# Deform stage of a four-layer convolution kernel: who copies the gather indices, and what GpSimd waits for between tiles

## The reference, cut to what matters

```python
offset = _conv2d(x, offset_w)                     # [B, 2*9, H, W]
sy = base_y + off[:, :, 0];  sx = base_x + off[:, :, 1]
y0, x0 = floor(sy), floor(sx);  ly, lx = sy - y0, sx - x0
p =     corner(y0,     x0,     (1 - ly) * (1 - lx))   # a gather per pixel and tap,
p = p + corner(y0,     x0 + 1, (1 - ly) * lx)         # zero outside the image
p = p + corner(y0 + 1, x0,     ly * (1 - lx))
p = p + corner(y0 + 1, x0 + 1, ly * lx)
y = jnp.einsum('bckhw,ock->bohw', p, wk)
attn = sigmoid(mean(y) + std(y));  return y * attn    # per image and channel
```

## Time and profile before

| what | before |
| --- | --- |
| median of three runs | 15070.81 us |
| the profiled execution's own time | 15021.82 us |
| its span | 15020.2 us |
| GpSimd busy, whole span | 7518.3 us (50%) |
| TensorE matmul, VectorE, ScalarE busy | 8857.2, 6520.5, 3085.6 us |
| indirect gathers (L1786) | 7056, 6823.6 us busy, 4426.0 us idle in front of them |
| granted TensorE clock, mean | 0.733 |

### The profile page before, as it was taken

The page is one execution under the profiler, slowest core; times in us unless marked ns, Lnnn a source line. Parts: engine busy times, 40 slices in busy tenths (PEclk is TensorE's granted clock), DMA queues, the critical chain, the costliest instruction groups (busy, mean ns, idle before and its releaser), DMA issues.

```text
span 15020.2 us, 156851 instructions
## 1 busy us (share of the span) xinstructions
PE 8857.2 (59%) x51639; PEld 6070.3 (40%) x51639; DVE 6520.5 (43%) x13120; ACT 3085.6 (21%) x5214; POOL 7518.3 (50%) x7657
## 2 busy tenths in 40 slices
PE   6897888888554544545454545454454545454543
PEld 2333444448443433333343434343343434343433
DVE  5655556553334444343434343434434343434333
ACT  3433444432111111111111111111111111111111
POOL 0011222212466666666666666666666666666665
PEclk9998999989666666767676766666666657676766
DMA  3322111126333333333333333333333333333332
GB/s 95 84 82 66 52 60 56 56 99 189 96 91 109 91 108 99 101 99 101 106 96 103 98 109 91 109 91 109 99 102 102 98 103 96 104 98 109 91 94 83
DMA packets 503924, 1436.05 MB, mean 96 GB/s; under 512 B 128980, under 2 KB 234196, under 8 KB 474576
## 3 DMA queue, kind: packets, MB, share of 16 engines
q0 software_dynamic: 353344, 970.88, 22.2%
q1 hardware_dynamic: 150032, 458.00, 10.1%
HBM read 1175.46 MB, written 252.90 MB: 95 GB/s over the span
## 4 chain that ended last, share of the span: by engine, by line
POOL 29%; issue 19%; DMA 13%; DVE 8%; PE 6%; another core or an unknown queue 0%; DVEq 0%; POOLq 0%; ACT 0%; ACTq 0%; SPq 0%
POOL e_g L1786 29%; DMA e_g<-table_dram,e_index_slots 12%; DVE e_g L2050 2%; PE e_ps L1903 2%; DVE e_g L2052 2%; PE e_ps L1918 2%; PE e_ps L1930 2%; PE e_ps L1939 1%; DMA e_tmp<-x3s_dram 1%; DVE e_x3t L1963 1%; DVE e_index_slots L2024 1%; DVE e_x3t L1967 0%; DVE e_w_next L2008 0%; DVE e_st L1971 0%
## 5 line engine op out<-in xcount | busy, mean ns | idle before, releaser
L1786 POOL DMA_INDIRECT e_g<-table_dram,e_index_slots x7056 | 6823.6, 967 | 4426.0 <-issue 1893.4
L1930 PE MATMUL e_ps<-k_ident,e_g 128*128 128x128 f32 x7056 | 1719.1, 398 | 4897.7 <-DVE e_g L2052 4840.2
L1930 PEld LDWEIGHTS e_ps<-k_ident,e_g 128*128 128x128 f32 x7056 | 1153.8, 197 | 5455.4 <-DVE e_g L2052 5209.6
L1939 PE MATMUL e_ps<-e_corners,e_w_def 128*64 128x128 f32 x14112 | 2667.5, 369 | 268.6 <-issue 148.9
L2024 DVE COPY e_index_slots<-e_index_now 128x9 uint32<-128x9 uint32 (+1 forms) x784 | 137.9, 177 | 5866.8 <-DMA e_g<-table_dram,e_index_slots 4314.5
L1939 PEld LDWEIGHTS e_ps<-e_corners,e_w_def 128*64 128x64 f32 x14112 | 2430.1, 197 | 463.7 <-issue 319.0
L1855 ACT ACTIVATE e_corners<-e_ps 128x512 f32<-128x512 f32 (+1 forms) x2352 | 1064.7, 489 | 4603.2 <-PE e_ps L1930 3895.9
L2049 DVE TENSOR_TENSOR e_ps<-e_g,e_ps 128x512 f32<-128x512 f32 (+1 forms) x2352 | 1324.5, 563 | 115.6 <-DMA e_g<-table_dram,e_index_slots 61.1
L2052 DVE TENSOR_TENSOR e_g<-e_g,e_ps 128x512 f32<-128x512 f32 (+1 forms) x2352 | 1301.5, 553 | 81.3
L2050 DVE TENSOR_TENSOR e_g<-e_g,e_ps 128x512 f32<-128x512 f32 (+1 forms) x2352 | 1284.8, 546 | 0.0
L1860 ACT ACTIVATE e_big<-e_ps 64x128 f32<-64x128 f32 (+1 forms) x784 | 211.8, 270 | 3518.7 <-remote 2210.0
(11 more groups left out here) (438 smaller groups left out, 8075.1 us busy)
## 6 DMA issues: line engine op xcount, KB each, us to landing
e_g<-table_dram,e_index_slots POOLq DMA_INDIRECT x7056
table_dram<-e_rt SPq DMA_DIRECT2D x32, 1624.0 KB
a_xt<-x_in SPq DMA_DIRECT2D x16, 1568.0 KB
v_dram<-a_vout SPq DMA_DIRECT2D x32, 784.0 KB, 8.5
b_xt<-v_dram SPq DMA_DIRECT2D x16, 1568.0 KB
v_dram<-b_vout SPq DMA_DIRECT2D x32, 784.0 KB, 7.5
c_v2t<-v_dram SPq DMA_DIRECT2D x16, 1568.0 KB
c_xt<-x_in SPq DMA_DIRECT2D x16, 1568.0 KB, 6.6
```

Source lines behind the costliest of these rows:

```text
L1786: pool.indirect_dma_start(out=g[:, slot, tap * CORNERS:(tap + 1) * CORNERS], out_offset=None, in_=table, in_offset=bass.IndirectOffsetOnAx ...
L1930: mm = pe.transpose(ps[:, TURN[tap // 4], (tap % 4) * P:(tap % 4 + 1) * P], g[:, slot, tap * CORNERS:tap * CORNERS + 2 * C], k.ident[:, :])
L1939: mm = pe.matmul(ps[0:C, OUT, 0:P], w_d[:, tap, :], corners[:, tap, :], start=(tap == 0), stop=(tap == TAPS - 1))
```

## The change

VectorE no longer copies indices. GpSimd has a new function, take: it copies the 9 indices of the tile itself, from index_now to index_slots, waits for its own copy (index_ready), and issues the nine gathers. The wait for the landing of the previous tile's gathers is gone. What used to follow from VectorE's copies is now said directly: GpSimd waits for bank_done of the tile that used the slot 7 tiles ago (as before), at a pair's first tile for the positions of that pair (switched at 3p), and after a pair's first group for the switch that follows the end of the pair before (switched at 3p + 2). GpSimd's one loop over 111 groups becomes a first group, a loop over the first pair's other groups, and a loop over the 15 other pairs with a loop over groups in it.

```diff
+                def take(r, slot, start):
+
+                    pool.tensor_copy(index_slots[:, slot, :], at(index_now, start, TAPS)).then_inc(index_ready, 1)
+                    pause(pool, index_ready, r * SLOTS + (slot + 1), passed)
+                    gather(slot)
+
+                pool.wait_ge(switched, 2)
                 for slot in range(SLOTS):
-                    pool.wait_ge(index_ready, slot + 1)
-                    if slot:
-                        pool.wait_ge(gathered[slot - 1], 16 * TAPS)
-                    gather(slot)
-                with pool.Fori(1, PAIRS * GROUPS) as r:
+                    take(0, slot, slot * TAPS)
+                with pool.Fori(1, GROUPS) as group:
                     for slot in range(SLOTS):
 
-                        pool.wait_ge(bank_done, (r - 1) * (3 * SLOTS) + (3 * slot + 3))
-                        pool.wait_ge(gathered[(slot - 1) % SLOTS], r * (16 * TAPS) + (16 * TAPS if slot else 0))
-                        pause(pool, index_ready, r * SLOTS + (slot + 1), passed)
-                        gather(slot)
+                        pause(pool, bank_done, (group - 1) * (3 * SLOTS) + (3 * slot + 3), passed)
+                        take(group, slot, group * GK + slot * TAPS)
+                with pool.Fori(1, PAIRS) as p:
+                    for slot in range(SLOTS):
+
+                        if slot == 0:
+                            pool.wait_ge(switched, p * 3)
+                        pause(pool, bank_done, (p * GROUPS - 1) * (3 * SLOTS) + (3 * slot + 3), passed)
+                        take(p * GROUPS, slot, K3 + slot * TAPS)
+                    pause(pool, switched, p * 3 + 2, passed)
+                    with pool.Fori(1, GROUPS) as group:
+                        for slot in range(SLOTS):
+
+                            pause(pool, bank_done, (p * GROUPS + group - 1) * (3 * SLOTS) + (3 * slot + 3), passed)
+                            take(p * GROUPS + group, slot, group * GK + slot * TAPS)
@@ positions, VectorE
                         switch(0)
-                        for slot in range(SLOTS):
-                            issue(slot, slot * TAPS)
@@ turn, VectorE
-                def issue(slot, start):
-
-                    dve.tensor_copy(index_slots[:, slot, :], at(index_now, start, TAPS)).then_inc(index_ready, 1)
@@
                         dve.wait_ge(gathered[slot], r * (16 * TAPS) + 16 * TAPS)
-                        if not last:
-                            issue(slot, group * GK + (GK + slot * TAPS))
```

## The result

The changed kernel takes 15874.01 us (median of four runs, 15852.92 to 15891.92) against 15067.99 us beside it: a ratio of 1.0536, with a 95% interval of 1.0518 to 1.0554. It is slower by 806 us where 1431 us were to be gained. The profiled execution took 15878.16 us, its span 15876.5.

A forecast was written before the change was run, and what follows sets the result against it. GpSimd was taken as the bound, by its nine gather issues and the pause between tiles. 15021.8 profiled - 2390 removed + 963 added = 13595, plus 49 for the runs' median: 13640 us, range 13010 to 14030.

The forecast's parts named there:

- What bounds before, and what the change removes: GpSimd's gathers and the pause between tiles bound the kernel; removing the landing wait at 783 steps saves 2390 us.
- What it adds: At each of 783 tile steps GpSimd now spends 1.23 us (0.42 to 1.70), in all 963 us.
- 0.15, 0.18 and 0.90 us: Parts of the new step: ninth gather's end to copy, the copy itself, copy's end to the next tile's first gather.
- The shared access to SBUF: VectorE instructions with two SBUF inputs could hold GpSimd's copies: nought in the sum, 16 us on the high end.
- What is late next. GpSimd still: After the change GpSimd takes 597 us a pair and stays last; VectorE's 280 and TensorE's 349 leave slack.
- The first, a landing wait in another form: GpSimd cannot issue past gathers in flight, so the step stays 3.05 us and the time 15070; chance 0.06.
- The second, the lead used up at a pair's end: GpSimd cannot get ahead at 15 pair ends, so 590 us return and the time is 14230; chance 0.05.
- The third: GpSimd pays 1.66 us per change between copy and gather; step 4.55 us, time 16245, slower; chance 0.05.
- What would show it: Gathers of 0.946 us spaced 1.25, steps near 1.2 alike everywhere, a copy near 0.2, VectorE still waiting for landings.
- two signs named for an error upward: In GpSimd's trace: the step exceeds 1.7 us, or gathers stretch while more than nine are in flight.

The follow-up runs named there:

- the kernel with four fills: Changed kernel plus four fills of 256 floats on GpSimd before each tile's copy; repeated over five runs: 14375.23 us, ratio 0.9517 to the kernel before.
- the first run with four fills: Changed kernel plus four fills of 256 floats on GpSimd before each tile's copy, measured the first time: 14348.39 us against 15082.36.
- the kernel before without any copy on GpSimd: Kernel before with GpSimd's wait for the previous tile's landing taken away, VectorE still copying the indices: 15954.09 us against 15042.58.
- the second probe: Kernel before plus, at its end, 180 TensorE records beside direct transfers from two queues, quarter-byte gathers and fills; 92 records in 10 us beside SyncE's transfers.
- the probe: Kernel before plus, at its end, 180 TensorE records beside gathers spaced by fills: pace breaks after 16 us at 1.33 us, 21 at 1.38, not at 1.44.

## Why the prediction was wrong, point by point

**What bounds before, and what the change removes: right.** GpSimd's step of 2.73 us was the bound, and it went. **What it adds: right within its ends.** Of 0.15, 0.18 and 0.90 us, in sum 1.23, the trace shows 0 (the copy starts where the ninth gather ends, 9042.78 + 0.96 = 9043.74), 0.20 and 0.81, in sum 1.01. **The shared access to SBUF** did not matter: a gather is 972 ns in the mean and was 967.

**The step that failed** is "What is late next. GpSimd still". It gave TensorE slack by its 349 us of busy time in a pair, a figure taken while the gathers came every 1.53 us in a usual tile. The change itself moved that to 1.34, and at 1.34 TensorE does not keep its pace: the changed kernel's gathers start from 3865.1 to 15820.0 us, 747 us a pair and not 597. So the sum was made for an engine that stays off the path, and the stage is now set by TensorE, through ScalarE (one weights bank for each group) and VectorE. GpSimd's gain is spent in its waits for bank_done. Why it comes out above the kernel before and not just level is argued from rows and not tried by itself: TensorE falls behind until GpSimd has filled its seven slots and stops, as it did for 28.98 us before 9031.66, and gets its pace back only in such stops; at 9058.15 it releases the next bank 2.33 us into GpSimd's idleness.

Could a row of the kernel before have warned? Of its timeline at the tile of the earlier trace rows, and, as the last row, the same matmuls of the kernel with four fills:

```profile
9022.56 3.02 PE L1939 MATMUL e_ps<-e_corners,e_w_def 128*64 128x128 f32 x18
9027.78 0.27 ACT L1860 ACTIVATE e_big<-e_ps 64x128 f32<-64x128 f32 x1 [4.56 <-remote]
...
9032.86 3.00 PE L1957 MATMUL e_ps<-e_corners,e_w_def 128*64 128x128 f32 x18
```

The matmuls of the kernel before are modelled to end at 9025.58; ScalarE is let go 2.20 us later, and the releaser is "remote". So a modelled end cannot be taken at its word. But that is no sign of a slowed TensorE yet: in the kernel with four fills, which keeps its pace, the modelled end is 9035.86 and ScalarE is let go at 9037.45, 1.59 us later. On the pages, "remote" ends 2210.0 of the 3518.7 us of idle time in front of this store before, 1996.6 of 3513.6 us in the first run with four fills, and 4534.7 of 5714.6 us in the changed kernel. The rows of before did not tell how TensorE fares at a faster rate; only a run could.

**The rivals.** The first, a landing wait in another form, did not come: the step is 1.01 us and the gathers run past those in flight. The second, the lead used up at a pair's end, is the nearest in kind, since the lead is used up again and again (VectorE's 73 waits for the next group's weights), but for another reason. The third ended on the right side by a wrong mechanism, which is luck: the step with both its changes is 1.01 us and not 4.55, and the kernel before without any copy on GpSimd is slower still. No rival had an engine slow down because another one issues faster, and 0.05 for slower was too little.

**What would show it.** The duration of 0.95, the spacing of 1.26 and the copy of 0.20 came as said. The step is alike only where nothing holds GpSimd, since 2523.6 us of idle time stand in front of the copies, and VectorE's waits for landings did not come. Of the two signs named for an error upward, stretched gathers did not come, and a step over 1.7 us came only as a wait for bank_done, which the prediction had put off the path.

The Trainium skill, SBUF — State Buffer, section Who interferes with whom, says that a transfer never contends with a compute engine and that TensorE and ScalarE never wait on anyone. Of direct transfers the second probe agrees (92 records in 10 us beside 248 GB/s). Of gathers the measurement differs, a record every 2.80 us, and the measurement decides; whether it is SBUF's ports that are held is not shown.

## What to carry to other kernels

An engine's slack is measured at the rate at which the others work now; where a change raises the rate of one engine's transfers, the slack of the others has to be measured at the new rate, best by a loop of their work beside such transfers. Where TensorE works beside a stream of GpSimd's gathers, find the interval at which it keeps its pace (here 1.44 us in the probe, 1.45 in the kernel) and issue no faster: 1.08 us of idle fills a tile were worth 9.4% against the changed kernel (14375 against 15874 us) and 4.8% against the one before. The sign is TensorE's records far ahead of those who wait for them (10.9 us here), with idle times that end at "remote" and grow with the change; the word alone is none, since about 2000 us of it stand in front of ScalarE's store in the best kernel too.

## What the runs showed of the hardware that was not expected

Gathers issued every 1.25 us slow TensorE, from 16 us after the first one, to records 0.7, 1.4, 2.1 and at last 2.80 us apart: multiples of 0.70. That depends neither on the bytes (64 or 256 floats a row) nor on the rows (64 or 128). Direct transfers of 128 KB from GpSimd's queue (one each 0.53 us, 248 GB/s), transfers from SyncE's queue and fills on GpSimd leave it alone. At 1.38 us the effect is late and mild at first, at 1.44 absent for as long as the probe looked (29 us).

That looks like something which each gather leaves behind, which takes about 1.40 us to work off, and which piles up if the gathers come faster; what it is stays open. The Trainium skill, DMA: Bandwidth & Descriptors, section Latency and other measured facts, has a guess at why two DMA engines, not TensorE, are slow: the descriptor rings of transfers from GpSimd lie in SBUF, and fetching from them makes ports busier. No run here shows that, and the direct transfers from the same queue, which did no harm, do not favour it. Nor was it tried whether only TensorE's weight loads, or its data, are slowed, and no run here tells whether TensorE is slowed as much in an execution that the profiler does not record.
